# Reciprocals of the softmax sums: from VectorE to GpSimd, as powers of minus one

## What is computed

```python
q_lr = jnp.einsum('bhtd,hdr->bhtr', q, Wq_lsr)
k_lr = jnp.einsum('bhtd,hdr->bhtr', k, Wk_lsr)
scores = jnp.einsum('bhir,bhjr->bhij', q_lr, k_lr) * scale
scores = jnp.where(causal_mask, jnp.float32(-jnp.inf), scores)
attn = jax.nn.softmax(scores, axis=-1)
y = jnp.einsum('bhij,bhjd->bhid', attn, v)
...
x = _layernorm(x + y @ Wo.T + bo)
```

## Time and profile before

| | |
|---|---|
| time, median of 3 runs | 3893.7 us (3890.47 to 3897.09) |
| the profiled execution's own time | 3893.05 us |
| its span | 3891.3 us |
| busy: TensorE, VectorE | 3630.7 us, 2260.8 us |
| busy: ScalarE, GpSimd | 1488.4 us, 666.7 us |
| granted TensorE clock, mean | 0.956 |
| TensorE waiting for VectorE or GpSimd, 910 to 1,190 us | 0.6 us |

### The profile page before, as it was taken

The page is one execution under the profiler, slowest core; times in us unless marked ns, Lnnn a source line. Parts: engine busy times, 40 slices in busy tenths (PEclk is TensorE's granted clock), DMA queues, the critical chain, the costliest instruction groups (busy, mean ns, idle before and its releaser), DMA issues. The chain is left out here.

```text
span 3891.3 us, 55460 instructions
## 1 busy us (share of the span) xinstructions
PE 3630.7 (93%) x19935; PEld 2505.5 (64%) x19935; DVE 2260.8 (58%) x4972; ACT 1488.4 (38%) x2793; POOL 666.7 (17%) x859
## 2 busy tenths in 40 slices
PE   4899999999999999999999737999999999999995
PEld 3555556556555555565555337888888888888884
DVE  2576665675765766657657475444444444544456
ACT  1253443443444434434434322333333333333335
POOL 2022121121121221211211201011111111111113
PEclk8999999999999999999999855999999999999997
DMA  5234234233323252332332203343343343444448
GB/s 169 61 93 127 76 92 123 62 97 112 102 72 113 79 142 64 101 110 71 89 115 66 72 0 99 100 139 117 112 131 111 120 124 111 130 121 117 143 157 308
DMA packets 207200, 423.14 MB, mean 109 GB/s; under 512 B 45840, under 2 KB 48912, under 8 KB 198800
## 3 DMA queue, kind: packets, MB, share of 16 engines
q1 hardware_dynamic: 180304, 367.47, 30.6%
q0 software_dynamic: 14400, 35.14, 4.6%
q10 hardware_dynamic: 12288, 17.83, 1.7%
HBM read 246.23 MB, written 72.38 MB: 82 GB/s over the span
## 5 line engine op out<-in xcount | busy, mean ns | idle before, releaser
L833 ACT ACTIVATE probs<-scores_t 128x512 f32<-128x512 f32 (+3 forms) x1536 | 656.8, 496 | 574.6 <-PE scores_t L700 516.9
L1801 PE MATMUL m_ps_h<-m_tokens_t,m_w_parts 128*128 128x512 f32 x3072 | 739.7, 391 | 1.6 <-DVE m_tokens_t L1683 1.6
L1801 PE MATMUL m_ps_y<-m_w_parts,m_hidden_parts 128*128 128x512 f32 x3072 | 737.3, 390 | 0.6
L1801 PEld LDWEIGHTS m_ps_y<-m_w_parts,m_hidden_parts 128*128 128x128 f32 x3072 | 575.3, 188 | 125.8 <-issue 6.3
L1801 PEld LDWEIGHTS m_ps_h<-m_tokens_t,m_w_parts 128*128 128x128 f32 x3072 | 575.3, 188 | 120.1 <-issue 2.0
L889 DVE CUSTOM_DVE_ANT_0 shared_banks<-shared_banks,mask_q_rows 128x128 f32<-128x128 f32 (+3 forms) x1024 | 477.7, 515 | 176.4 <-PE shared_banks L657 173.9
L657 PE MATMUL shared_banks<-k_operands,q_operands 96*128 96x512 f32 (+3 forms) x1536 | 509.3, 379 | 23.7 <-DVE natural L880 8.9
L700 PE MATMUL scores_t<-q_operands,k_operands 128*128 128x512 f32 (+3 forms) x1536 | 494.7, 372 | 33.3 <-ACT probs L833 26.1
L1619 ACT ACTIVATE m_hidden<-m_ps_h,m_b 128x512 f32<-128x512 f32 x256 | 176.6, 690 | 791.1 <-PE m_ps_h L1801 777.9
L562 POOL TENSOR_SCALAR_AFFINE_SELECT probs<-probs 128x256 f32<-128x256 f32 x512 | 220.3, 433 | 1341.3 <-ACT probs L833 1340.7
L657 PEld LDWEIGHTS shared_banks<-k_operands,q_operands 96*128 96x128 f32 x1536 | 279.0, 191 | 263.7 <-issue 122.9
(11 more groups left out here) (243 smaller groups left out, 3225.2 us busy)
## 6 DMA issues: line engine op xcount, KB each, us to landing
m_w_raw<-in_w1T SPq DMA_DIRECT2D x64, 1024.0 KB, 5.2
m_w_raw<-in_w2T SPq DMA_DIRECT2D x64, 1024.0 KB, 7.5
wqk_group<-scratch_wqk SPq DMA_DIRECT2D x32, 1024.0 KB, 5.6
q_operands<-natural SPq DMA_DIRECT2D x192, 128.0 KB, 2.6
k_operands<-natural SPq DMA_DIRECT2D x192, 128.0 KB, 2.7
q_operands<-natural SPq DMA_DIRECT2D x384, 64.0 KB, 2.0
k_operands<-natural SPq DMA_DIRECT2D x384, 64.0 KB, 2.0
natural<-in_xT SPq DMA_DIRECT2D x8, 2048.0 KB, 9.8
```

The lines of the kernel that those rows point to most:

```text
L833: act.activation(probs[:, slot_of(k, h // 2), h % 2, c0:HALF], st[:, (HG * k + h) % SCORE_BANKS, c0:HALF], ACT.Exp, scale=SCALE).then_inc( ...
L1801: mm = pe.matmul(bank, a, b, start=(first and n == 0), stop=(final and n == len(pairs) - 1))
```

## The change

GpSimd inverts the pieces of `den` itself, at the places where VectorE did: it raises each element to the power of minus one, with a column of minus ones, broadcast, as the second operand. VectorE's reciprocals and their semaphore `rden_ready` go; `inverted` takes its place, and `invert` on GpSimd waits for VectorE's copy (`den_drained`). Nothing else moves.

```diff
+        minus = sb("minus_one", [P, 1])
...
+            pool.memset(minus[:], -1.0)
...
+            def invert(b, g, hh, piece):
+
+                n = 2 * (b * GROUPS + g) + hh
+                width = HALF // DEN_PIECES
+                cols = slice(piece * width, (piece + 1) * width)
+
+                pool.wait_ge(den_drained, n + 1)
+                pool.tensor_tensor(den[:, cols], den[:, cols], minus[:].to_broadcast([P, width]), ALU.pow
+                                   ).then_inc(inverted, 1)
+
...
-                pool.wait_ge(rden_ready, DEN_PIECES * (n + 1))
+                pool.wait_ge(inverted, DEN_PIECES * (n + 1))
                 pool.tensor_tensor(half, half, den[:], ALU.mult).then_inc(normed, 1)
...
+                    if item[0] == "invert":
+                        invert(b, *item[1:])
                     if item[0] == "invert" and item[3] == DEN_PIECES - 1:
                         normalise(b, item[1], item[2])
...
                     if kind == "invert":
-                        invert(b, *item[1:])
                         continue
...
-                dve.wait_ge(den_drained, n + 1)
-                dve.reciprocal(den[:, cols], den[:, cols]).then_inc(rden_ready, 1)
```

More of the change, by code:

```diff
@@ L344, in build_attention @@
         st_full, exp_done, pv_done, normed = sem("st_full"), sem("exp_done"), sem("pv_done"), sem("normed")
-        y_drained, den_drained, rden_ready = sem("y_drained"), sem("den_drained"), sem("rden_ready")
+        y_drained, den_drained, inverted = sem("y_drained"), sem("den_drained"), sem("inverted")
         mx_joined, mneg_hi, m_sent = sem("mx_joined"), sem("mneg_hi"), sem("m_sent")
```

## The result

The kernel now takes 8,340.1 us (8,338.4 to 8,341.9, 4 runs) against 3,893.7: the ratio is 2.142 [2.138, 2.146]. The profiled span is 8,338.8 us, 4,447.5 more than before.

The account below looks back on a forecast made before the run. TensorE was taken to bound the kernel. Its added idle time of 360 us, plus 96 us for the clock, less 3 us gained, made 453 us on 3,893: 4,346 us, range 3,900 to 5,400.

Parts of the forecast that it names:

- the price of one power: GpSimd's time X for one 128x128 power: 4.0 us, assuming fifteen arithmetic steps; range 0.32 to 9 us.
- rival 1: GpSimd pays only its usual ratio to VectorE, 1.86, so a power takes 1.74 us: 3,935 us; chance 0.24.
- GpSimd becomes the bound: Rival 2: a power takes over 6 us; at 8 us the kernel takes 5,175 us; chance 0.22.
- What bounds the kernel, and what is removed: Attention stage: TensorE sets the pace; removing VectorE's 256 reciprocals, 235.5 us, gains only about 3 us.
- rival 3: The cover holds: with a power below 1.08 us nothing waits, 3,890 us; chance 0.12.
- Slot starts: Masks queue behind four powers: TensorE idles 9.2 us at each start of slots 1 and 2, 11.7 at slot 3.
- Lower halves: Last powers ahead of the k = 9 masks: 3.3 us together in slots 0 and 1, 1.7 in slot 3.
- 22X - 45.1: TensorE's added idle us in a middle batch, for X above 4.2; 42.9 us was taken at X = 4.
- Tail: Three powers ahead of the output bias additions: first layer norm 10.4 us later, 4.6 hidden, 5.8 us a middle batch.
- The lock: Powers hold up VectorE's layer norm passes in the tail: 2 us a tail, up to about 4 by the skill's rule.
- The clock: After waits TensorE's granted clock falls to 0.5: four clusters a batch, 12 us each batch, 96 us in all.
- The signs that I named: Changed profile: mask waits some 290 us, GpSimd busy up 256X, about 1,020 us; row maxima and expert stage unchanged.

Follow-up runs that it names:

- the multiply: The changed kernel with each power replaced by a multiply with the column of minus ones, sums not inverted: 3,888.1 us, ratio 0.9991.
- 11 columns: The changed kernel with each power on only the first 11 of its 128 columns, the rest left uninverted: 3,991.6 us, ratio 1.026.
- 25 columns: The changed kernel with each power on only the first 25 of its 128 columns, the rest left uninverted: 4,349.7 us, ratio 1.117.
- 64 columns: The changed kernel with each power on only the first 64 of its 128 columns, the rest left uninverted: 5,746.9 us, ratio 1.477.

## Why the prediction was wrong

**The step that failed** is the price of one power: "I take X = 4.0 us (an estimate, fifteen steps at 0.27 us) and keep 0.32 to 9 us for the range". It measured 20.72. The upper bound had been made of the same assumption as the value, a number of passes of a GpSimd that does 1.7 to 2.5 ns a column; the runs show 159 ns a column, with no regard to the exponent or the number of rows. With no row of the trace for the operation, thirty-odd passes were no bound but a second guess. The ratio of 1.86 behind rival 1 was that of a multiply to an addition and says nothing of the power, which stands to the reciprocal as 22. Even the lower bound was off a little: a multiply of 128 columns takes 0.40 us, and not a quarter of the 1,285 ns of 512 columns, 0.32. Of the rivals, "GpSimd becomes the bound" is what happened, at a price beyond its own.

**What bounds the kernel, and what is removed**: right. The gain from VectorE was put at 3 us; the multiply shows 0 to 7 (ratio 0.9982 to 1.0000). Its price lies below 1.08 us, and TensorE waits once for a mask, 1.6 us (before once, 2.5): rival 3 is how the kernel behaves at that price.

**Slot starts**: right, at four values of X. For slots 1 and 2 the intervals are 12.7, 21.1, 45.9 and 86.7 us (11, 25, 64 and 128 columns), by the formula 12.6, 21.4, 46.2 and 87.0; for slot 3, from the end of the drain, 11.2, 20.1, 44.9 and 85.7 us, by the formula 11.4, 20.2, 45.0 and 85.8.

**Lower halves**: right in place, wrong as a formula for a large X. I had counted only the two last pieces, with the first two hidden behind the four blocks without masks. These traces show the lower half of slot 1, before and after:

```profile
1006.64 0.68 DVE L867 COPY denominators<-den_bank 128x512 f32<-128x512 f32 x1
...
1033.99 0.85 PE L719 MATMUL y_bank<-probs,v_rows 128*32 128x384 f32 x8
```

```profile
2809.18 0.69 DVE L880 COPY denominators<-den_bank 128x512 f32<-128x512 f32 x1 [17.22 <-PE den_bank L733]
2809.96 41.40 POOL L574 TENSOR_TENSOR denominators<-denominators,minus_one 128x128 f32<-128x128 f32 x2 [1.98 <-DVE denominators L880]
...
2852.14 1.93 PE L733 MATMUL y_bank<-probs,v_rows 128*32 128x512 f32 x8 [18.20 <-POOL probs L564]
...
2895.57 1.51 PE L733 MATMUL y_bank<-probs,v_rows 128*32 128x384 f32 x8 [38.32 <-POOL probs L564]
```

Two powers, 41.40 us together, no longer fit ahead of k = 8, so all four count: 86.4 us against 27.4, an excess of 59 and not of the 35 that 2X + 2.1 - 8.44 gives. At 64 columns this begins. In slot 1 of batch 3 the product of k = 8 does not wait, but its masks end 22.5 us behind the drain's start, 18.9 before, and the third power can only follow them: the product of k = 9 comes 45.6 us behind the drain, an excess of 18.3 where the formula has 14.7.

**The batch, worked out again with X = 20.72.** Starts of slots 1 and 2: 76.1 each; of slot 3: 78.6; lower halves 59 in each of four slots: 236; tail 3X - 6.2 = 55.9. Together 523 us. TensorE is busy 293 us longer in all, 37 a batch: its matmuls run at 1.2 GHz more often. That makes 560, and the batch became 554 longer. Eight times 554 is nearly the whole difference. The prediction says that 22X - 45.1 holds "above 4.2"; by its own terms it holds up to 4.2, and above that slot 2's k = 9 adds 2X - 8.4, as in rival 2. With the right X the prediction's formulas give 22X - 45.1 + 33 (slot 2's k = 9) = 444 a batch and, with the clock's 293 us, some 7,750 us in all: of the error of 3,994 us some 3,400 are the price, and most of the rest is the two pieces thought hidden.

**Tail**: right in size. The first layer norm is 60.6 us late, by the terms of the prediction 60.5, and TensorE waits 55.9 us.

**The lock**: wrong, and small. I had taken 2 us a tail for VectorE's passes held up by a power. They are not: the pass of two inputs of the layer norm (L948) takes 750, 752 and 754 ns (least, median, most of 64), and 16 of them ran wholly inside a power. So did all 14 of VectorE's subtractions of two tiles (L873, before L860), at 1.22 us each, where beside masks they had taken 1.42 to 1.64 us. One of the 16:

```profile
3358.86 20.73 POOL L574 TENSOR_TENSOR denominators<-denominators,minus_one 128x128 f32<-128x128 f32 x1
...
3361.02 0.75 DVE L948 SCALAR_TENSOR_TENSOR probs<-probs,rms_inverse,norm_weight 128x512 f32<-128x512 f32 x1
```

The rule drawn from the Trainium skill (SBUF — State Buffer, "Who interferes with whom"), a lock held for a whole instruction, would have made L948 up to 20 us here. The trace doesn't agree for the power.

**The clock**: right in kind, too low in size. In a stretch of the attention stage of the changed kernel it is 0.66 on average. At 25 columns TensorE is busy 137 us longer than before, and I had 96 at X = 4 for the loss by clock. The granted clock falls to 0.5 eight to ten times a batch there (once before, once or twice with 11 columns), and I had counted four. The waits' own sum was too high (400 without the lock, against 344, and 325 of idle time). These two errors and the lock's 16 us partly cancel, and the piece was dearer than 4.0: that the kernel of 25 columns comes within 4 us of 4,346 is luck.

**The signs that I named**: GpSimd's busy time by 256X, that is 5,304 us: it rose by 5,267. Waits for masks: 2,961 us and not 290; they grow with X, and faster than it. The row maxima kept their times (512 columns: 723 ns, before 721). The expert stage is as before.

## What to carry to other kernels

An operation that no trace shows got no upper bound by analogy here; measure one of it, or give the range a tail of another order of magnitude, above all for a function (power, logarithm, exponential) on an engine whose rows show only additions, masks and products. The place of the work, on the other hand, could be read beforehand: compare the in-order queue of the engine that gets it, from its first possible start to the last mask behind it, with the time that its consumer spent there before, and count every piece, also those that seem hidden, since cover has a length. And to relieve an engine that the bound engine hardly waits for brings about what its waits say (2.5 us), at the risk of all that stands behind the work in its new place.

## What the runs showed of the hardware

- A power on GpSimd (tensor_tensor, fp32) costs 0.36 us and 159 ns a column, for 32 rows as for 128, for the exponent 2 as for -1; the multiply of the same 128 columns costs 0.40 us.
- A power did not hold VectorE up, and an addition of GpSimd did. In the kernel of 25 columns a pass of one input (L939) takes 1.56 to 1.59 us in the eight cases, one a batch, in which it starts together with GpSimd's bias addition, and 0.53 to 0.54 in the other 56, also inside a power (3360.35 in the changed kernel):

```profile
1059.62 1.58 DVE L939 TENSOR_SCALAR probs<-probs,ln_mv,ln_rstd 128x512 f32<-128x512 f32 x1
1059.64 1.27 POOL L601 TENSOR_TENSOR x_residual<-x_residual,bo_folded 128x512 f32<-128x512 f32 x1
```

```profile
3360.35 0.54 DVE L939 TENSOR_SCALAR probs<-probs,ln_mv,ln_rstd 128x512 f32<-128x512 f32 x1
```
